# Two-batch macaron block on one core: later max and exponential units, and VectorE adding probability tiles ahead of the softmax sums

## The chip, the cores and the metric

The kernel runs on one core of a Trainium2 chip. The metric is the device time of one execution in microseconds (us); the kernel before is given as the median of three runs. TensorE does the matrix products, VectorE, ScalarE and GpSimd the work between them, and SyncE's queue issues the DMAs.

## The reference

Input x is (2, 1024, 512) in float32. Three residual steps follow each other: half a feed-forward step, attention, and another half feed-forward step, each on a layer-normalised x.

```python
x = x + 0.5 * ffn(layernorm(x), weight, bias, gamma, beta)   # inner layernorm, ternary weight
x = x + attn(layernorm(x), w_q, w_k, w_v, w_o)
x = x + 0.5 * ffn(layernorm(x), weight, bias, gamma, beta)

def attn(x, ...):                       # 16 heads of 32, rotary q and k
    scores = einsum('bhqd,bhkd->bhqk', q, k) / sqrt(32)
    scores = where(tok_mask, scores, -inf)     # causal in blocks of 64 tokens
    ctx = einsum('bhqk,bhkd->bhqd', softmax(scores), v)
    return ctx @ w_o.T
```

## The kernel before, in words

**Groups and runs.** The 16 heads of a batch form 4 groups of 4 heads, 8 groups in all. Every engine walks through one written-out loop over steps `k`; 48 steps make a run, and one run holds, side by side, one stage of three different groups:

- the q and k projections of group g (four parts of 12 steps, the products at their first ten steps, `L956`); ScalarE copies each result to `t1` one step after the last product (`L602`), GpSimd rotates it with four operations (`L502` twice, `L505`, `L507`), ScalarE and GpSimd split it into a high and a low half (`L623` at lag 8, `L511` at lag 9), and SyncE writes it to DRAM and reads it back into `qst` or `kst` (lags 11 and 14);
- the max pass of group g-1, "A units" from step `A_START` of the run on: 48 score products (`L939`), one a step, 12 for each head, each reduced over keys by VectorE (`L815`). They rotate through three PSUM banks (`a_bank`), so that a product waits until the unit three before it is reduced. After the twelfth unit of a head VectorE makes the max row with three small operations, each waiting for the one before: `L825` (min of two slices of `rmax`), `L827` (scaled high half) and `L828` (low half). I call these three **the max chain**. `MAX_PLACE` steps later TensorE transposes the result into one of the same three banks (`L1063`), ScalarE copies it one step later (`L617`), and a DMA puts it into `qst`. Around that place two A units have only two banks between them.
- the exponential pass of group g-2, "B units" from `B_START` on: 48 score products in transposed order (`L920`) over two banks, each turned into probabilities by ScalarE (`L609`). They form 12 steps of keys `st` with four heads each; `st` 0 to 3 belong to the first half of the queries and have 512, 384, 256 and 128 columns, `st` 4 to 7 to the second half with 512 columns each (the full tiles), `st` 8 to 11 again 512, 384, 256 and 128. `probs` has four places, so a tile lives for four values of `st`.

**Sums and contexts.** Five steps after its first unit (`SUM_LAG`), TensorE adds each `st` into the softmax sum with a ones matrix (`L1045`), for four heads in f32; nine steps after it (`PV_LAG`) it multiplies the same probabilities with v (`L1055`). So every fourth step has an f32 **block**: sums of one `st` and contexts of the one before. When the last `st` of a half is through, ScalarE takes the reciprocal by a logarithm and an exponential (`L629`, `L633`), VectorE multiplies (`L834`), and ScalarE and GpSimd split the result (`L641`, `L521`).

**Order.** Inside step k TensorE issues: B unit, A unit, projection, (other products), f32 block, transpose of the max row. VectorE issues: A reduction, then, where it is due, the max chain, then `L834`. Waits are on semaphores that count these operations. The third stage ends after 8 groups; the output products of batch 0 and its last feed-forward step are set between the last units, and those of batch 1 follow.

Of the kernel before, what the change touches and what calls it, by code (L numbers as in the profile page):

```python
# [17 lines left out]
F32 = mybir.dt.float32  # L18
# [29 lines left out]

STEPS = 48
ALL = BATCH * GROUPS  # L50
A_START, B_START = 10, 18
SUM_LAG, PV_LAG = 5, 9
P_PLACES = 4

SLOTS = [(0,), (1,), (2,), (3,), (4, 5), (6,), (7,), (8,), (9,), (10, 11)]
MAX_PLACE = 2
A_ORDER = [(i, half) for i in range(TILES) for half in range(i // 4 + 1)]
A_UNITS = len(A_ORDER)
B_ORDER = [(half, j) for half in range(BLOCKS) for j in range(4 * half + 4)]
# [7 lines left out]
def macaron(nc, x, w_q, w_k, w_v, w_o, w_f, bias, gamma, beta, cos_t, sin_t, ident_in, ident16_in,  # L67
            q_rows, k_rows, spread, out):
    ctx = ExitStack()
    with ctx:  # L70
# [69 lines left out]
        wf_s = flat(cl, None)  # L140
        wtg = xl[:, 0:2, :].rearrange("p a t -> p (a t)").rearrange("p (a b) -> p a b", a=4)

        x1_dram = [dram(f"x1_{b}", (P, TILES, C), F32) for b in range(BATCH)]
        xh_dram, xl_dram = dram("xh_1", (P, CC, T), F16), dram("xl_1", (P, CC, T), F16)
        ch_dram, cl_dram = dram("ch_0", (P, GROUPS, T), F16), dram("cl_0", (P, GROUPS, T), F16)
# [69 lines left out]
        s_qb = sem("s_qb")  # L215
        s_eb = sem("s_eb")
        s_sum = sem("s_sum")
        s_pv = sem("s_pv")
        s_ln = sem("s_ln")
        s_rec = sem("s_rec")  # L220
# [72 lines left out]
        def pv_step(k, lag):  # L293

            t = b_unit(k - lag)
            return (t[0], t[1], *t[3:]) if t and t[2] == 0 else None

        def ctx_half(k, lag=1):

# [23 lines left out]
        def _(sp):  # L323
# [64 lines left out]
            for k in range(LAST_STEP):  # L388
# [12 lines left out]
                if u := proj_after(k, 14):  # L401
# [4 lines left out]
                    if g >= SETS:  # L406
                        sp.wait_ge(s_qb, STEPS * (g - SETS + 1))
                    sp.dma_start(dst[0:MASK_ROW, g % SETS, :, cols],
                                 spread[n % 2].rearrange("a (d h) t -> (a d) h t", h=GH)).then_inc(s_stack[m], 16)
                if e := max_head(k, 4):  # L410
                    g, h = e
                    n = GH * g + h
                    sp.wait_ge(s_mrows, n + 1)
                    sp.dma_start(qst[MAX_ROW:ROWS_B, g % SETS, h, :], mrows[:, n % 2, :]).then_inc(s_mdma[h], 16)
# [113 lines left out]
        def _(act):  # L528
# [52 lines left out]
            for k in range(LAST_STEP):  # L581
# [21 lines left out]
                if t := b_unit(k):  # L603
                    g, st, h, half, j, q0, n = t
                    u = STEPS * g + GH * st + h
                    act.wait_ge(s_qb, u + 1)
                    if 12 * g + st >= P_PLACES:
                        act.wait_ge(s_pv, 12 * g + st + 1 - P_PLACES)
                    nc.scalar.activation(probs[:, st % P_PLACES, h, 0:n], pb[u % 2][:, 0:n], ACT.Exp,  # L609
                                         scale=EXP_SCALE).then_inc(s_eb, 1)  # L610
                if e := max_head(k, 3):
                    n = GH * e[0] + e[1]
                    act.wait_ge(s_mtr, n + 1)
                    if n >= 2:
                        g2, h2 = divmod(n - 2, GH)
                        act.wait_ge(s_mdma[h2], (g2 + 1) * 16)
                    nc.scalar.activation(mrows[:, n % 2, :], max_bank(n)[0:2 * TILES, 0:P // 2].bitcast(F16), ACT.Copy).then_inc(s_mrows, 1)  # L617
# [5 lines left out]
                    nc.scalar.activation(rhl[:, n % 2, 0, :], t1[:, n % 2, :], ACT.Copy).then_inc(s_rh, 1)  # L623
                if c := ctx_half(k, -4):
                    n = 2 * c[0] + c[1]
                    act.wait_ge(s_sum, 12 * c[0] + 4 + 8 * c[1])
                    if n:
                        act.wait_ge(s_cl, n)
                    nc.scalar.activation(cf[:, :], psum[:, :], ACT.Ln).then_inc(s_ln, 1)  # L629
# [16 lines left out]
        def _(dve):  # L646
# [126 lines left out]
            for k in range(LAST_STEP):  # L773
# [45 lines left out]
                if e := max_head(k, 0):  # L819
# [3 lines left out]
                    if n >= 2:  # L823
# [3 lines left out]
                    link(nc.vector.tensor_scalar(mparts[:, s, 0, :], rmax[:, at:at + 8], 1.0 / MAX_SCALE, None, ALU.mult))  # L827
                    nc.vector.scalar_tensor_tensor(mparts[:, s, 1, :], rmax[:, at:at + 8], 1.0 / MAX_SCALE,  # L828
                                                   mparts[:, s, 0, :], ALU.mult, ALU.subtract).then_inc(s_mp, 1)
                if c := ctx_half(k, 1):  # L830
                    n = 2 * c[0] + c[1]
                    dve.wait_ge(s_rec, n + 1)
                    dve.wait_ge(s_pv, 12 * c[0] + 4 + 8 * c[1])
                    nc.vector.scalar_tensor_tensor(cf[:, :], acc[:, :], CTX_SCALE, cf[:, :], ALU.mult, ALU.mult).then_inc(s_cf, 1)  # L834
# [20 lines left out]
        def _(pe):  # L855
# [52 lines left out]
            for k in range(LAST_STEP):  # L908
# [126 lines left out]
                if t := pv_step(k, SUM_LAG):  # L1035
                    g, st, half, j, q0, n = t
                    pe.wait_ge(s_eb, STEPS * g + GH * (st + 1))
                    if st == 0 and g % GROUPS == 0:
                        pe.wait_ge(s_vs[g // GROUPS], TILES)
                    if j == 0 and (g or half):  # L1040
                        pe.wait_ge(s_ln, 2 * g + half)
                    if g == 0 and st == 0:
                        pe.wait_ge(s_vs[1], TILES)
                    for h in range(GH):
                        last = nc.tensor.matmul(psum[h * D:(h + 1) * D, q0 - half * HALF:HALF], ones[:, 0:D],  # L1045
                                                probs[:, st % P_PLACES, h, 0:n], start=(j == 0), stop=(j == 4 * half + 3),
                                                skip_group_check=True)
                    last.then_inc(s_sum, 1)
                if t := pv_step(k, PV_LAG):
                    g, st, half, j, q0, n = t  # L1050
                    if j == 0 and (g or half):
# [8 lines left out]
                if e := max_head(k, MAX_PLACE):  # L1060
                    n = GH * e[0] + e[1]
                    pe.wait_ge(s_mp, n + 1)
                    nc.tensor.transpose(max_bank(n)[0:2 * TILES, 0:P // 2].bitcast(F16),  # L1063
                                        mparts[:, n % 2, :, :].rearrange("p a t -> p (a t)"),
                                        ident16[:, :]).then_inc(s_mtr, 1)
# [87 lines left out]
```

## Time and profile before

| what | value |
|---|---|
| median of 3 runs | 634.64 us (634.29 to 636.09) |
| the profiled execution | 634.23 us, its span 632.4 us |
| mean granted TensorE clock | 0.962 |
| TensorE busy | 554.8 us (88%) |
| VectorE busy | 396.8 us (63%) |
| ScalarE busy | 310.2 us (49%) |
| GpSimd busy | 238.5 us (38%) |

Busy is the time in which an engine had an instruction under way. Products are pipelined on TensorE, and the profile models their ends, so that the distance from one product's start to the next one's tells more of its cost than its own length. About 1.8 us of the execution lie around the span.

### The profile page before, as it was taken

To read this page: it belongs to the slowest core of one execution; us is meant where nothing else is said; L and a number is where in the kernel's file an instruction comes from. 1 tells how busy PE (TensorE), PEld (TensorE's weight loads), DVE (VectorE), ACT (ScalarE), POOL (GpSimd) and SP (SyncE) were. 2 spreads that over 40 slices of the span, in tenths; PEclk is the share of its full clock that TensorE was granted. 3 is DMA by queue.
4 is the path that set the end of the run, shared out by engine and by line. 5 is a ranking of instruction groups with operands and counts; after the bars stand their busy time and mean duration, and the time that the engine had idled before them with its cause. 6 is when DMAs were issued, how large, how long until landed. Compare 5 with 4: busy or idle time off the path is not lost.

```text
span 632.4 us, 10042 instructions
## 1 busy us (share of the span) xinstructions
PE 554.8 (88%) x3586; PEld 235.9 (37%) x3586; DVE 396.8 (63%) x782; ACT 310.2 (49%) x629; POOL 238.5 (38%) x200
## 2 busy tenths in 40 slices
PE   0695799679969999999999999999999898999876
PEld 0442445334423333333333333333333334344432
DVE  5899656626767757757757657657657843431672
ACT  0931632121215746746746746746736548572320
POOL 4001363443474646646646646646600100000100
PEclk9796899888989999999999999999999999999997
DMA  8921023354221215423213214514410003100011
GB/s 322 348 76 68 2 70 97 117 119 133 93 83 51 77 52 175 127 67 110 76 51 109 77 52 150 169 51 143 138 57 2 1 2 134 51 18 34 33 68 66
DMA packets 43601, 57.95 MB, mean 92 GB/s; under 512 B 3526, under 2 KB 34374, under 8 KB 42528
## 3 DMA queue, kind: packets, MB, share of 16 engines
q1 hardware_dynamic: 42972, 57.21, 27.6%
q8 instruction: 29, 0.48, 0.3%
q10 hardware_dynamic: 580, 0.11, 0.1%
q14 instruction: 20, 0.16, 0.1%
HBM read 32.01 MB, written 25.17 MB: 90 GB/s over the span
## 4 chain that ended last, share of the span: by engine, by line
PE 56%; DVE 19%; issue 8%; POOL 7%; DMA 7%; ACT 3%; SPq 1%; ACTq 0%; POOLq 0%; DVEq 0%
PE bank L956 9%; PE bank L874 7%; PE bank L939 7%; PE bank L920 7%; PE bank L1045 6%; PE bank L1055 5%; PE bank L884 5%; PE bank L993 5%; DMA kst<-spread 4%; DVE rmax L815 4%; DVE mparts L828 3%; DVE stats L661 3%; POOL rot L502 2%; DMA spread<-rhl 2%; PE bank L864 2%
## 5 line engine op out<-in xcount | busy, mean ns | idle before, releaser
L815 DVE TENSOR_REDUCE rmax<-bank 128x1 f32<-128x512 f32 (+3 forms) x384 | 200.9, 553 | 124.5 <-PE bank L939 121.5
L609 ACT ACTIVATE big<-bank 128x512 f32<-128x512 f32 (+3 forms) x384 | 182.0, 490 | 150.6 <-PE bank L920 145.7
L939 PE MATMUL bank<-kst,qst 104*128 104x512 f16 (+3 forms) x384 | 126.3, 330 | 15.3 <-issue 8.5
L920 PE MATMUL bank<-qst,kst 106*128 106x512 f16 (+3 forms) x384 | 123.9, 330 | 2.5 <-ACT big L609 2.2
L502 POOL TENSOR_TENSOR rot<-t,sin_s 64x512 f32<-64x512 f32 x64 | 81.8, 1277 | 96.3 <-ACT t L602 93.5
L1045 PE MATMUL bank<-big,ones 128*32 128x512 f32 (+3 forms) x768 | 81.8, 498 | 0.0
L1055 PE MATMUL bank<-big,rows 128*32 128x512 f32 (+3 forms) x768 | 79.5, 486 | 0.0
L920 PEld LDWEIGHTS bank<-qst,kst 106*128 106x128 f16 x384 | 37.1, 97 | 84.4 <-issue 41.4
L511 POOL TENSOR_TENSOR rhl<-t,rhl 128x512 f16<-128x512 f32 x32 | 37.5, 1171 | 70.9 <-ACT rhl L623 70.9
L521 POOL TENSOR_TENSOR cl<-cf,ch 128x512 f16<-128x512 f32 x16 | 18.6, 1160 | 112.3 <-ACT ch L641 112.3
L939 PEld LDWEIGHTS bank<-kst,qst 104*128 104x128 f16 x384 | 37.8, 98 | 51.2 <-issue 18.9
L956 PE MATMUL bank<-xh,wh 128*128 128x512 f16 x128 | 50.9, 401 | 6.4 <-DVE xl L697 5.9
L956 PE MATMUL bank<-xl,wh 128*128 128x512 f16 x128 | 44.9, 392 | 0.0
L461 POOL TENSOR_TENSOR rstd<-var_e,half_neg 128x4 f32<-128x4 f32 x12 | 13.0, 1084 | 83.5 <-DVE var_e L670 83.5
L956 PE MATMUL bank<-xh,wl 128*128 128x512 f16 x128 | 43.6, 381 | 0.0
L507 POOL TENSOR_TENSOR t<-t,rot 128x512 f32<-128x512 f32 x32 | 41.2, 1286 | 2.5
L505 POOL TENSOR_TENSOR t<-t,cos_s 128x512 f32<-128x512 f32 x32 | 40.9, 1280 | 2.5
L1055 PEld LDWEIGHTS bank<-big,rows 128*32 128x32 f32 x768 | 24.5, 110 | 37.5 <-issue 34.7
L690 DVE SCALAR_TENSOR_TENSOR rows<-bank,rows 128x512 f32<-128x512 f32 x24 | 16.3, 689 | 35.0 <-PE bank L874 34.8
L543 ACT ACTIVATE xh<-bank,bet,gam 128x512 f16<-128x512 f32 x24 | 18.9, 787 | 35.9 <-PE bank L864 35.9
L828 DVE SCALAR_TENSOR_TENSOR mparts<-rmax,mparts 128x8 f16<-128x8 f32 x32 | 34.6, 1081 | 1.1
L623 ACT ACTIVATE rhl<-t 128x512 f16<-128x512 f32 x32 | 20.0, 626 | 20.5 <-POOL t L507 20.5
(106 smaller groups left out, 667.9 us busy)
## 6 DMA issues: line engine op xcount, KB each, us to landing
spread<-rhl SPq DMA_DIRECT2D x32, 256.0 KB, 2.2
qst<-spread SPq DMA_DIRECT2D x16, 384.0 KB, 3.8
kst<-spread SPq DMA_DIRECT2D x16, 384.0 KB, 3.8
x<-rows SPq DMA_DIRECT2D x4, 1024.0 KB, 4.6
spread<-rhl SPq DMA_DIRECT2D x32, 128.0 KB, 2.1
rows<-in_L_attn_x_dram SPq DMA_DIRECT2D x3, 1024.0 KB, 15.5
xh<-ch SPq DMA_DIRECT2D x4, 512.0 KB, 4.6
xl<-cl SPq DMA_DIRECT2D x4, 512.0 KB, 6.2
```

The lines of the kernel that those rows point to most:

```text
L502: pool.tensor_tensor(rot[first:first + P // 2, n % 2, :], t1[other:other + P // 2, n % 2, :], sin_s[other:other + P // 2, cols], ALU.mult) ...
L505: pool.tensor_tensor(t1[:, n % 2, :], t1[:, n % 2, :], cos_s[:, cols], ALU.mult).then_inc(s_rot, 1)
L507: pool.tensor_tensor(t1[:, n % 2, :], t1[:, n % 2, :], rot[:, n % 2, :], ALU.add).then_inc(s_rope, 1)
L609: nc.scalar.activation(probs[:, st % P_PLACES, h, 0:n], pb[u % 2][:, 0:n], ACT.Exp, scale=EXP_SCALE).then_inc(s_eb, 1)
L815: nc.vector.tensor_reduce(rmax[:, at:at + 1], a_bank(u)[:, 0:n], AX.X, ALU.max, negate=True).then_inc(s_max, 1)
L828: nc.vector.scalar_tensor_tensor(mparts[:, s, 1, :], rmax[:, at:at + 8], 1.0 / MAX_SCALE, mparts[:, s, 0, :], ALU.mult, ALU.subtract).then ...
L874: last = nc.tensor.matmul(dst[:, :], (high, low)[a][:, cc, r * P:(r + 1) * P], wt[:, cc, :], start=False, stop=(n == 2 * CC))
L920: nc.tensor.matmul(pb[u % 2][:, 0:n], kst[0:ROWS_B, g % SETS, h, j * P:(j + 1) * P], qst[0:ROWS_B, g % SETS, h, q0:q0 + n], start=True, st ...
L939: nc.tensor.matmul(a_bank(u)[:, 0:n], qst[0:ROWS_A, g % SETS, h, i * P:(i + 1) * P], kst[0:ROWS_A, g % SETS, h, half * HALF:half * HALF + ...
L956: last = nc.tensor.matmul(pp[:, :], wp[ww][:, m % 2, cc, og * P:(og + 1) * P], xp[xw][:, cc, m // 2 * HALF:(m // 2 + 1) * HALF], start=(n ...
L1045: last = nc.tensor.matmul(psum[h * D:(h + 1) * D, q0 - half * HALF:HALF], ones[:, 0:D], probs[:, st % P_PLACES, h, 0:n], start=(j == 0), s ...
L1055: last = nc.tensor.matmul(acc[h * D:(h + 1) * D, q0 - half * HALF:HALF], rows[g // GROUPS][:, j, (GH * og + h) * D:(GH * og + h + 1) * D], ...
```

## The change

`A_START` goes from 10 to 11, `B_START` from 18 to 22, `MAX_PLACE` from 2 to 5. Of the full key tiles, `st` 4 and 5, and `st` 6 and 7, are added in pairs: VectorE writes probs[st] + probs[st+1] for each of the four heads (f32, 128 x 512) into `added`, which lies over the value weights that are no longer needed; the four additions of a pair come at lags 7, 8, 9 and 10 after the first unit of `st` 4 or 6. TensorE sums the totals instead of the four single tiles, at the lag of `st` 6 and of `st` 8. ScalarE waits for the additions before it overwrites their tiles.

```diff
-A_START, B_START = 10, 18
+A_START, B_START = 11, 22
+PAIRED = (4, 6)
+ADD_LAGS = (7, 8, 9, 10)
+SUMS = 10
-MAX_PLACE = 2
+MAX_PLACE = 5
+        added = [part[:, 2, :, :].rearrange("p c o -> p (c o)").bitcast(F32).rearrange("p (h n) -> p h n", h=2) for part in (wh, wl)]
+        def add_unit(k):
+            for h, lag in enumerate(ADD_LAGS):
+                s = pv_step(k, lag)
+                if s and s[1] in PAIRED:
+                    return s[0], PAIRED.index(s[1]), s[1], h
 # sync: max row out
-                if e := max_head(k, 4):
+                if e := max_head(k, MAX_PLACE + 2):
 # scalar
+                    if 4 <= st - P_PLACES < 8:
+                        act.wait_ge(s_add, 8 * g + 4 * ((st - P_PLACES - 4) // 2) + 4)
-                if e := max_head(k, 3):
+                if e := max_head(k, MAX_PLACE + 1):
-                    act.wait_ge(s_sum, 12 * c[0] + 4 + 8 * c[1])
+                    act.wait_ge(s_sum, SUMS * c[0] + 4 + (SUMS - 4) * c[1])
 # vector, behind the max chain of the step
+                if t := add_unit(k):
+                    g, p, st, h = t
+                    dve.wait_ge(s_eb, STEPS * g + GH * (st + 1) + h + 1)
+                    if g == 0 and p == 0:
+                        dve.wait_ge(s_vs[1], TILES)
+                    elif p == 0:
+                        dve.wait_ge(s_sum, SUMS * (g - 1) + 6)
+                    else:
+                        dve.wait_ge(s_sum, SUMS * g + 5)
+                    nc.vector.tensor_tensor(added[h // 2][:, h % 2, :], probs[:, st % P_PLACES, h, :],
+                                            probs[:, (st + 1) % P_PLACES, h, :], ALU.add).then_inc(s_add, 1)
 # tensor
-                    if j == 0 and (g or half):
-                        pe.wait_ge(s_ln, 2 * g + half)
-                    for h in range(GH):
-                        last = nc.tensor.matmul(psum[...], ones[:, 0:D], probs[:, st % P_PLACES, h, 0:n], start=(j == 0), ...)
-                    last.then_inc(s_sum, 1)
+                    if st - 2 in PAIRED:
+                        p = PAIRED.index(st - 2)
+                        pe.wait_ge(s_add, 8 * g + 4 * p + 4)
+                        if p == 0:
+                            pe.wait_ge(s_ln, 2 * g + 1)
+                        for h in range(GH):
+                            last = nc.tensor.matmul(psum[h * D:(h + 1) * D, :], ones[:, 0:D], added[h // 2][:, h % 2, :],
+                                                    start=(p == 0), stop=False, skip_group_check=True)
+                        last.then_inc(s_sum, 1)
+                    if st == 0 and g:
+                        pe.wait_ge(s_ln, 2 * g)
+                    if st < 4 or st >= 8:
+                        for h in range(GH):
+                            last = nc.tensor.matmul(psum[...], ones[:, 0:D], probs[:, st % P_PLACES, h, 0:n], start=(st == 0), ...)
+                        last.then_inc(s_sum, 1)
 # tensor, at the transpose of the max row
+                    if n + 1 < GH * ALL:
+                        pe.wait_ge(s_max, A_UNITS * (n + 1) + MAX_PLACE - 2)
```

## Rows read from the trace of the kernel before

**Rows 1.** Page, part 1: busy time, share, instructions.

```profile
PE 554.8 (88%) x3586; PEld 235.9 (37%) x3586; DVE 396.8 (63%) x782; ACT 310.2 (49%) x629; POOL 238.5 (38%) x200
```

**Rows 2.** Windows: PE, PEld, DVE, ACT, POOL busy; clock; DMA share; GB/s.

```profile
286.70:334.00 47.30, 45.55 (x342) 17.90 (x341) 32.03 (x63) 29.57 (x67) 27.19 (x22) 1.00 0.25 79
476.00:523.40 47.40, 45.28 (x339) 16.68 (x331) 31.12 (x72) 26.19 (x60) 3.34 (x3) 1.00 0.02 4
523.40:570.80 47.40, 45.24 (x307) 19.24 (x307) 17.02 (x32) 33.12 (x63) 3.34 (x3) 1.00 0.16 65
```

**Rows 3.** TensorE timeline, run 286.7 to 334: start us, length us, instruction, idle before.

```profile
286.92 0.38 PE L939 MATMUL bank<-kst,qst 104*128 104x512 f16 x1
287.14 0.59 PE L956 MATMUL bank<-xh,wl 128*128 128x512 f16 x2
287.57 0.33 PE L920 MATMUL bank<-qst,kst 106*128 106x384 f16 x1
287.74 0.22 PE L939 MATMUL bank<-kst,qst 104*128 104x128 f16 x1
...
289.05 0.40 PE L1055 MATMUL bank<-big,rows 128*32 128x128 f32 x8
289.80 0.22 PE L1063 MATMUL bank<-ident,mparts 128*16 128x128 f16 x1 [0.35 <-DVE mparts L828]
...
299.40 0.61 PE L1055 MATMUL bank<-big,rows 128*32 128x256 f32 x8
300.69 0.22 PE L1063 MATMUL bank<-ident,mparts 128*16 128x128 f16 x1 [0.67 <-DVE mparts L828]
...
307.34 1.07 PE L1045 MATMUL bank<-big,ones 128*32 128x512 f32 x8
308.22 1.04 PE L1055 MATMUL bank<-big,rows 128*32 128x512 f32 x8
309.20 0.39 PE L920 MATMUL bank<-qst,kst 106*128 106x512 f16 x1
...
328.01 0.38 PE L939 MATMUL bank<-kst,qst 104*128 104x512 f16 x1 [0.69 <-DMA kst<-spread]
```

**Rows 4.** VectorE timeline, same run.

```profile
286.68 1.35 DVE L815 TENSOR_REDUCE rmax<-bank 128x1 f32<-128x512 f32 x2 [0.99 <-PE bank L939]
288.06 0.16 DVE L825 TENSOR_TENSOR rmax<-rmax 128x4 f32<-128x4 f32 x1
288.26 0.17 DVE L827 TENSOR_SCALAR mparts<-rmax 128x8 f16<-128x8 f32 x1
288.46 1.28 DVE L828 SCALAR_TENSOR_TENSOR mparts<-rmax,mparts 128x8 f16<-128x8 f32 x1
...
290.97 0.68 DVE L834 SCALAR_TENSOR_TENSOR cf<-bank,cf 128x512 f32<-128x512 f32 x1
291.57 1.48 DVE L815 TENSOR_REDUCE rmax<-bank 128x1 f32<-128x512 f32 x3
...
333.97 0.69 DVE L815 TENSOR_REDUCE rmax<-bank 128x1 f32<-128x512 f32 x1 [0.99 <-PE bank L939]
```

**Rows 5.** ScalarE timeline, same run.

```profile
287.77 0.60 ACT L602 ACTIVATE t<-bank 128x512 f32<-128x512 f32 x1
```

**Rows 6.** GpSimd timeline, same run.

```profile
288.44 2.61 POOL L502 TENSOR_TENSOR rot<-t,sin_s 64x512 f32<-64x512 f32 x2 [2.65 <-ACT t L602]
```

**Rows 7.** Line L828 over the whole span: ns min/median/max, first and last start.

```profile
L828 DVE SCALAR_TENSOR_TENSOR mparts<-rmax,mparts x32: 168/1278/1290, 151.2 to 516.7; 128x8 f16<-128x8 f32 x32
```

**Rows 8.** VectorE timeline, 70 to 100 us.

```profile
77.12 1.03 DVE L684 TENSOR_TENSOR cl<-big,ch 128x512 f16<-128x512 f32 x1 [0.65 <-ACT big L544]
```

**Rows 9.** GpSimd timeline, 70 to 100 us.

```profile
74.49 3.11 POOL L502 TENSOR_TENSOR rot<-t,sin_s 64x512 f32<-64x512 f32 x2 [7.93 <-ACT t L602]
77.68 1.59 POOL L505 TENSOR_TENSOR t<-t,cos_s 128x512 f32<-128x512 f32 x1
```

**Rows 10.** VectorE timeline, 108 to 125 us.

```profile
117.37 5.81 DVE L676 TENSOR_SCALAR kst<-rows,mv,rstd 128x512 f32<-128x512 f32 x4 [1.21 <-POOL rstd L461]
```

More of the change, by code:

```diff
@@ L217, in macaron @@
         s_sum = sem("s_sum")
+        s_add = sem("s_add")
         s_pv = sem("s_pv")
@@ L1039, in _ @@
                         pe.wait_ge(s_vs[g // GROUPS], TILES)
-                    if j == 0 and (g or half):
-                        pe.wait_ge(s_ln, 2 * g + half)
                     if g == 0 and st == 0:
                         pe.wait_ge(s_vs[1], TILES)
-                    for h in range(GH):
-                        last = nc.tensor.matmul(psum[h * D:(h + 1) * D, q0 - half * HALF:HALF], ones[:, 0:D],
-                                                probs[:, st % P_PLACES, h, 0:n], start=(j == 0), stop=(j == 4 * half + 3),
-                                                skip_group_check=True)
-                    last.then_inc(s_sum, 1)
+                    if st - 2 in PAIRED:
[11 more added lines that the diff above has]
+                        for h in range(GH):
+                            last = nc.tensor.matmul(psum[h * D:(h + 1) * D, q0 - half * HALF:HALF], ones[:, 0:D],
+                                                    probs[:, st % P_PLACES, h, 0:n], start=(st == 0), stop=(j == 4 * half + 3),
+                                                    skip_group_check=True)
+                        last.then_inc(s_sum, 1)
                 if t := pv_step(k, PV_LAG):
```

## The prediction

> **What bounds the kernel now.** I read the page's totals first: TensorE is busy 88% of the span, VectorE 63%, GpSimd 38% [rows 1]. Then windows of one run each: from 192 us to 429 us the runs repeat, TensorE at 45.5 of 47.3 us and full clock, VectorE at 32, GpSimd at 27 [rows 2]. The same reduction comes back 47.29 us later (286.68, 333.97) [rows 4]. Six such runs hold B units of groups 0 to 5 beside projections; the last two B groups have no projection beside them, and GpSimd is idle there (3.3 us of 47.4) [rows 2].
>
> In the TensorE timeline nearly all starts follow each other without a hole: 0.22 us for 512 f16 columns (286.92 to 287.14), so 0.17, 0.11 and 0.06 for 384, 256 and 128, and 0.88 us for four f32 sums of 512 columns (307.34 to 308.22) [rows 3], 0.22 for each 128. I see two sorts of holes. The transpose of the max row waits for the max chain: the block part at 289.05 takes 0.22, the transpose starts at 289.80, a hole of 0.5; the one at 299.40 takes 0.44, the transpose is at 300.69, a hole of 0.85; the other two heads of the run have next to none. And one A unit waits 0.7 us for `kst` [rows 3]. A run has 2.1 us of holes, and else is TensorE work: 45.2 us.
>
> **Removed sums.** Four sums of 0.88 become two: -1.76 us a run of TensorE's own work, on the path.
>
> **Removed waits.** The transpose moves from two steps behind the last A unit to five, and over a further block: its 1.4 us go. `A_START` gives the `kst` DMA one more step of about 0.9 us: its 0.7 us go (the fixed chain from projection to landing isn't shortened; were it late again, up to 0.7 comes back). Together with the sums: -3.85 us a run, if nothing new is late.
>
> **The additions by themselves.** 128x512 f32 from two SBUF operands isn't in the trace; the nearest are the same operation with an f16 operand (L684) and L834, 0.68 us, the next instruction 0.60 after its start [rows 4]. I take 0.60; 8 a run are 4.8 us on an engine with 15 us free a run. As a sum this costs nothing. It is covered only where VectorE keeps within three A units of TensorE, so I look at the place.
>
> **What holds VectorE.** L828 handles 8 elements and takes 168 ns at the least, but 1278 in the median [rows 7]. At 288.46 it starts 20 ns after a GpSimd operation of 1.27 us (half of the 2.61 from 288.44 [rows 6]) and ends with it, at 289.74 [rows 4]. L684, a 512-column operation on two SBUF tensors, starts at 77.12 under a GpSimd operation that ends at 77.60, and ends 0.55 us behind that, at 78.15 [rows 8, 9]; the GpSimd operation that starts at 77.68 then takes 1.59 instead of 1.27 [rows 9]. Four L676 under the same GpSimd sequence take 5.81 us, one GpSimd operation each [rows 10]. L834 and L815, which read PSUM, aren't held (0.68 at 290.97, under GpSimd) [rows 4, 6]. So: a VectorE operation with two SBUF operands that starts under a GpSimd operation waits for its end, then streams.
>
> GpSimd's four rotations start with ScalarE's copy, one step behind the last projection product (287.77 + 0.60 + 0.07 = 288.44) [rows 5, 6], and last 5.3 us (four of 1.27, gaps of 0.08 [rows 9]). In the kernel before the first two operations of the max chain are through by then (288.06, 288.26) and only L828 is held [rows 4]. Afterwards the last A unit comes one step later against the projection, about 0.8 us (0.65 for the products of the step from 286.92, 0.17 for the next B unit) [rows 3]. L825 then starts 0.4 us inside the first rotation. It waits for its end (289.7), L827 slips in ahead of the second rotation (which comes after a gap of 0.08, while L827 is ready after 0.06: 0.02 as L828 ended behind the rotation, 0.04 as between L825's end and L827's start [rows 4, 6]), and L828 is held to the second one's end, about 291.1 instead of 289.74.
>
> L825 handles 4 elements, and in this trace it never meets a running rotation. The Trainium skill ("GPSIMD Engine Reference", section Key points) says that GpSimd shares its SBUF interfaces with VectorE and contends with instructions that have two SBUF inputs. By that L825 is held too; the trace bears the rule out for L684 and L828, and shows nothing for L825. By the rule the sum is the one below, without it that of the second rival.
>
> **The four head boundaries of a run.** I lay them out from step 12h+9's start, with the widths above, 0.1 us on either side of a block, ScalarE's copy and the rotations as read. The fourth A unit of the new head needs its first one reduced, and that stands behind the chain.
> - Head 0 to 1: TensorE could issue the fourth unit at 3.7 (block 0.7); last unit reduced 2.0, L825 held to 2.9, L828 to 4.2, first unit reduced 4.45: a hole of 0.75.
> - Head 1 to 2: the same with 3.55 against 4.4: 0.85.
> - Head 2 to 3, where the first pair's additions lie at the steps of the last two A units and of the first two new ones. From step 44's start: `L834` ends 1.67, unit 10 reduced 2.27, addition 0 at once (the rotation of 2.4 now waits for it and ends 4.1), unit 11 reduced 3.55, L825 held to 4.1, L828 to 5.45, addition 1 streams to 6.05, unit 0 reduced 6.3 (TensorE wanted it at 4.7: 1.6). Addition 2 is held by the third rotation to 7.7, unit 1 reduced 8.05 (TensorE at 7.0: 1.0), addition 3 held by the fourth to 9.3, and the pair's sums, ready at 8.5, wait 0.8 for it. Holes of 3.4.
> - Head 3 to 4: the second pair's additions meet only one GpSimd operation (L511), and the block there has two sums and a context, 2.6 us, which cover the chain but for 0.5.
>
> Together 5.5 us. From below: 2.5, if L825 isn't held and only the additions are; 0.8, if neither is (VectorE's own work at boundary 2). From above: L827 held as well adds one rotation, 1.35, at each of four boundaries: 10.9. I take 5.5, since L684 is the closest row to both operations.
>
> **Sum.** A run: -3.85 + 5.5 = +1.65, times six = +10. The two last B groups have no rotations: -1.76 each in windows where TensorE is busy 45.3 of 47.4 us [rows 2]: -3. At the start four more steps have A units without B units, where a step goes by the reduction's 0.69 instead of TensorE's 0.44 (1.0), and the chain is a little longer in the heads before: +1 in all; the four more steps at the end hold no new work. All other edits (SyncE's lag of the max row, ScalarE's waits for additions some ten steps old) have slack: cost 0; with the slack gone a late max row would hold the first B unit. Sum +8 on the profiled execution of 634.23: 642, where the median is 634.64.
>
> **Rivals.**
> 1. *The chain runs into the rotations and additions wait* (above): 642. Slower from holes of 4.2 us a run on (3.85 plus the ends' share). Its own range is 637 to 651.
> 2. *L825 isn't held, the additions are.* The chain ends as before, 0 at boundaries 0, 1 and 3, 2.2 at boundary 2 (0.2, 1.1 and 0.9 by the same list), 0.3 for the second pair: -3.85 + 2.5 = -1.35, times six -8, -3, +1: 624. For it: 4 elements. Against: L828's 8 are held.
> 3. *Nothing is held long* (TensorE's steps let VectorE meet gaps): -3.85 + 0.8 times six, -18, -3, +1: 614. Against it the order of L828 and the rotation, alike in most of its 32 places.
> 4. *It evens out*: holes of about 4.1 us a run, as with one addition less held: 634.
> 5. *L827 is held too*: +5.4 a run, 32 us more: 674. Against: it is ready 20 ns ahead of the rotation.
>
> **Numbers.** Chances: 0.47 for the first, 0.24 for the second, 0.12 for the third, 0.11 for the fourth, 0.06 for the fifth (slower). A part of the first's low end falls within 0.3%. A measurement of this kernel tells about 0.3% from no change: faster 0.37, within 0.12, slower 0.51. The range 615 to 651 leaves out the fifth and most of the third.
>
> **What the profile would show.** Of the six sums of 512 columns (L1045, times four heads) in a run, four are left; there are 64 additions. L825's mean well over 0.16 us, up to 1; L828's still over 1 in runs with GpSimd, and its end some 2.6 us behind the rotations' start. Additions of the first pair at 0.7 to 1.5 us, of the last two groups at 0.69. TensorE's waits: none for L828 at the transpose, none for `kst`; new ones for L815 at L939 and for the addition at L1045. Runs of about 49 us. I am wrong if L825 keeps 0.16 us under a running rotation, if `kst` is late again, or if runs come down to 44 us.

## The result and the profile after

664.46 us (median of 4, 664.25 to 668.63) against 634.46 us: 1.0492 times the time of the kernel before, 95% interval 1.0469 to 1.0516. Slower, as forecast, but by 30 us and not by 8, and above the range's upper end of 651. The rows below are from one profiled execution of each kernel (664.37 and 634.23 us).

The page of the changed kernel: totals, the clock's line of tenths by slice, the chain by engine, and the group of A units. (Lines have moved: `L967` is the A unit, `L948` the B unit, `L842`, `L844` and `L845` the max chain, `L856` the additions, `L1076` the sums of totals, `L1083` the other sums, `L1093` the contexts, `L517`, `L520`, `L522` the rotations, `L526` the split of the rotated tile, `L536` the context's low half.)

```profile
PE 556.7 (84%) x3458; PEld 233.9 (35%) x3458; DVE 457.9 (69%) x846; ACT 308.5 (47%) x629; POOL 251.5 (38%) x200
...
PEclk9897999789979899899899899899999899999798
...
PE 59%; DVE 29%; issue 6%; ACT 3%; DMA 1%; POOL 1%; SPq 0%; ACTq 0%; DVEq 0%; POOLq 0%
...
L967 PE MATMUL bank<-kst,qst 104*128 104x512 f16 (+3 forms) x384 | 126.5, 332 | 39.3 <-DVE rmax L832 32.3
```

Against [rows 1], VectorE's busy time went up by 61 us, though 64 additions at 0.69 are 44. TensorE's went up by 2 us though 128 of its instructions are gone, and in the steady part the clock's line has an 8 every third slice or so. A units wait 32 us for reductions.

One steady run, from a view of windows (PE, PEld, DVE, ACT, POOL busy, clock, DMA share, GB/s), and the two us at a time around its head boundary 2 to 3:

```profile
253.50:304.70 51.20, 45.87 (x328) 17.44 (x324) 40.67 (x70) 29.33 (x66) 29.31 (x23) 0.97 0.30 93
266.00:268.00 2.00, 0.61 (x3) 0.21 (x3) 2.00 (x4) 0.53 (x1) 1.92 (x2) 1.00 1.04 299
268.00:270.00 2.00, 0.83 (x4) 0.11 (x2) 2.00 (x3) 0.60 (x1) 1.92 (x3) 1.00 0.93 315
270.00:272.00 2.00, 1.42 (x9) 0.50 (x13) 2.00 (x4) 0.00 (x0) 1.49 (x1) 0.73 0.22 75
272.00:274.00 2.00, 2.00 (x14) 0.46 (x7) 0.14 (x1) 0.00 (x0) 0.00 (x0) 0.50 0.00 0
274.00:276.00 2.00, 2.00 (x10) 0.88 (x11) 0.85 (x2) 1.48 (x4) 0.00 (x0) 0.92 0.00 0
```

A run takes 51.2 us, not 47.3 [rows 2]. For four us VectorE and GpSimd are busy all the time and TensorE 1.44 us; then TensorE's clock goes down to half (1.2 GHz of 2.4) for 3.4 us. That happens once in each of the five runs that hold B groups 0 to 4. The DMA share near 1 in these rows isn't part of it: at the same boundary of the first of these runs (215 to 219 us) the share is 0.18, and TensorE is busy 1.43 us of the 4, with the clock at half behind it.

VectorE's and GpSimd's timelines there (start, length, instruction):

```profile
263.34 0.68 DVE L856 TENSOR_TENSOR wh<-big 128x512 f32<-128x512 f32 x1
263.94 0.68 DVE L832 TENSOR_REDUCE rmax<-bank 128x1 f32<-128x512 f32 x1
264.65 0.53 DVE L842 TENSOR_TENSOR rmax<-rmax 128x4 f32<-128x4 f32 x1
265.22 0.17 DVE L844 TENSOR_SCALAR mparts<-rmax 128x8 f16<-128x8 f32 x1
265.42 1.11 DVE L845 SCALAR_TENSOR_TENSOR mparts<-rmax,mparts 128x8 f16<-128x8 f32 x1
266.46 0.68 DVE L856 TENSOR_TENSOR wh<-big 128x512 f32<-128x512 f32 x1
267.06 0.28 DVE L832 TENSOR_REDUCE rmax<-bank 128x1 f32<-128x128 f32 x1
267.26 1.55 DVE L856 TENSOR_TENSOR wl<-big 128x512 f32<-128x512 f32 x1
268.73 0.41 DVE L832 TENSOR_REDUCE rmax<-bank 128x1 f32<-128x256 f32 x1
269.06 1.41 DVE L856 TENSOR_TENSOR wl<-big 128x512 f32<-128x512 f32 x1
```

```profile
263.43 3.08 POOL L517 TENSOR_TENSOR rot<-t,sin_s 64x512 f32<-64x512 f32 x2 [1.90 <-ACT t L617]
266.59 1.67 POOL L520 TENSOR_TENSOR t<-t,cos_s 128x512 f32<-128x512 f32 x1
268.34 1.59 POOL L522 TENSOR_TENSOR t<-t,rot 128x512 f32<-128x512 f32 x1
269.89 1.60 POOL L536 TENSOR_TENSOR cl<-cf,ch 128x512 f16<-128x512 f32 x1
```

`L842` has 4 elements and takes 0.53 us, until the first rotation ends; `L844` slips in; `L845` waits for the second; the third addition for the third, the fourth for the last one. GpSimd loses time in turn: the operations beside additions last about 1.6 us, where rotations take 1.27 and `L536` takes 1.16 elsewhere. And TensorE, from which one reads the bill:

```profile
265.52 0.38 PE L948 MATMUL bank<-qst,kst 106*128 106x512 f16 x1
267.39 0.39 PE L967 MATMUL bank<-kst,qst 104*128 104x512 f16 x1 [1.50 <-DVE rmax L832]
...
269.20 0.39 PE L967 MATMUL bank<-kst,qst 104*128 104x512 f16 x1 [0.98 <-DVE rmax L832]
...
270.58 0.79 PE L1076 MATMUL bank<-wh,ones 128*32 128x512 f32 x2 [0.78 <-issue]
...
271.95 2.01 PE L1093 MATMUL bank<-big,rows 128*32 128x512 f32 x8
273.66 0.31 PE L1103 MATMUL bank<-ident,mparts 128*16 128x128 f16 x1
```

Measured from start to start, less each product's own length at full clock, the holes are 1.66, 1.14 and 0.94 us. The contexts from 271.95 take 1.71 us where they take 0.88 elsewhere, the sums before them 1.37 instead of 0.85. The three holes, the slow stretch behind them (1.75 us in all) and the holes of the other boundaries (1.0, 1.1 and 0.8) are 8.4 us; the kernel before had 2.5 by the same measure. 8.4 - 2.5 - 1.76 of sums = +4.1; the run is 3.9 longer.

**Where the 30 us are.** From the starts of the B groups in both timelines, each group up to the start of the next: group 0 starts as before (189.8 against 189.7), groups 0 to 4 longer by 19.8, group 5 by 0.8, group 6 by 2.5, group 7 by 5.3 (62.3 against 57.0), and behind the last B unit 1.7 (55.1 against 53.4).

Group 5 is worth a look. The first pair meets the rotations there as in groups 0 to 4: `L842` 0.53, `L845` 1.11, additions of 1.55 and 1.42 us at 472.18 and 473.98. But the output products of batch 0 have taken the place of the projections, TensorE is busy 1.86 us of 4 (471.3 to 475.3) and not 1.44, it waits 1.06, 0.77 and 0.56 us and not 1.50, 0.98 and 0.78, and the clock stays at full speed. The group is 0.8 us longer, groups 0 to 4 are 3.8 to 4.3 us longer.

### The profile page after: what moved, and what is told of

It is laid out like the page before. It is cut to its first block, busy times and chain, and to the rows that moved or that the text cites. A ratio compares the mean times of both kernels' runs of the same rounds, so it can differ in the third digit from the quotient of the medians.

```text
span 662.6 us, 9960 instructions
## 1 busy us (share of the span) xinstructions
PE 556.7 (84%) x3458; PEld 233.9 (35%) x3458; DVE 457.9 (69%) x846; ACT 308.5 (47%) x629; POOL 251.5 (38%) x200
## 4 chain that ended last, share of the span: by engine, by line
PE 59%; DVE 29%; issue 6%; ACT 3%; DMA 1%; POOL 1%; SPq 0%; ACTq 0%; DVEq 0%; POOLq 0%
PE bank L984 9%; PE bank L1093 8%; PE bank L967 7%; PE bank L948 7%; DVE rmax L832 7%; PE bank L902 6%; PE bank L912 6%; PE bank L1083 6%; PE bank L1021 5%; DVE stats L678 3%; PE bank L1076 3%; DVE mparts L845 3%; DVE wl L856 3%; DVE rmax L842 3%; PE bank L892 2%
## 5 line engine op out<-in xcount | busy, mean ns | idle before, releaser
L832 DVE TENSOR_REDUCE rmax<-bank 128x1 f32<-128x512 f32 (+3 forms) x384 | 199.5, 550 | 89.4 <-PE bank L967 88.2
L967 PE MATMUL bank<-kst,qst 104*128 104x512 f16 (+3 forms) x384 | 126.5, 332 | 39.3 <-DVE rmax L832 32.3
L948 PE MATMUL bank<-qst,kst 106*128 106x512 f16 (+3 forms) x384 | 127.5, 334 | 3.6 <-ACT big L626 3.3
L517 POOL TENSOR_TENSOR rot<-t,sin_s 64x512 f32<-64x512 f32 x64 | 86.3, 1348 | 82.2 <-ACT t L617 79.5
L1093 PE MATMUL bank<-big,rows 128*32 128x512 f32 (+3 forms) x768 | 85.7, 516 | 1.4 <-DVE cf L862 1.4
L526 POOL TENSOR_TENSOR rhl<-t,rhl 128x512 f16<-128x512 f32 x32 | 38.5, 1204 | 90.7 <-ACT rhl L640 90.7
L948 PEld LDWEIGHTS bank<-qst,kst 106*128 106x128 f16 x384 | 37.1, 97 | 94.7 <-ACT big L626 35.7
L967 PEld LDWEIGHTS bank<-kst,qst 104*128 104x128 f16 x384 | 38.0, 99 | 86.5 <-DVE rmax L832 43.4
L536 POOL TENSOR_TENSOR cl<-cf,ch 128x512 f16<-128x512 f32 x16 | 21.8, 1365 | 99.0 <-ACT ch L658 99.0
L1083 PE MATMUL bank<-big,ones 128*32 128x128 f32 (+3 forms) x512 | 47.7, 443 | 0.0
L520 POOL TENSOR_TENSOR t<-t,cos_s 128x512 f32<-128x512 f32 x32 | 43.3, 1354 | 2.5
L522 POOL TENSOR_TENSOR t<-t,rot 128x512 f32<-128x512 f32 x32 | 43.0, 1344 | 2.5
L1093 PEld LDWEIGHTS bank<-big,rows 128*32 128x32 f32 x768 | 24.0, 113 | 34.8 <-issue 31.6
L617 ACT ACTIVATE t<-bank 128x512 f32<-128x512 f32 x32 | 19.1, 598 | 26.9 <-PE bank L984 26.6
L845 DVE SCALAR_TENSOR_TENSOR mparts<-rmax,mparts 128x8 f16<-128x8 f32 x32 | 30.9, 965 | 1.1
```

The costliest lines, as they stand in the source:

```text
L517: pool.tensor_tensor(rot[first:first + P // 2, n % 2, :], t1[other:other + P // 2, n % 2, :], sin_s[other:other + P // 2, cols], ALU.mult) ...
L520: pool.tensor_tensor(t1[:, n % 2, :], t1[:, n % 2, :], cos_s[:, cols], ALU.mult).then_inc(s_rot, 1)
L522: pool.tensor_tensor(t1[:, n % 2, :], t1[:, n % 2, :], rot[:, n % 2, :], ALU.add).then_inc(s_rope, 1)
L832: nc.vector.tensor_reduce(rmax[:, at:at + 1], a_bank(u)[:, 0:n], AX.X, ALU.max, negate=True).then_inc(s_max, 1)
L948: nc.tensor.matmul(pb[u % 2][:, 0:n], kst[0:ROWS_B, g % SETS, h, j * P:(j + 1) * P], qst[0:ROWS_B, g % SETS, h, q0:q0 + n], start=True, st ...
L967: nc.tensor.matmul(a_bank(u)[:, 0:n], qst[0:ROWS_A, g % SETS, h, i * P:(i + 1) * P], kst[0:ROWS_A, g % SETS, h, half * HALF:half * HALF + ...
```

## The experiments

The diffs show the lines that carry each edit; counters and waits that follow from them are left out. A ratio is to the kernel before, with its 95% interval.

The held theory says: VectorE operations on two SBUF tensors wait for GpSimd's operations; that, above all where the first pair's additions stand beside the rotations, opens TensorE's holes, and the clock goes down behind them. Its rivals: the additions cost by their own length (work); the three new places cost by themselves (place).

### One part of the change alone

`e1_shift_only`: the kernel before with the three places.

```diff
-A_START, B_START = 10, 18
+A_START, B_START = 11, 22
-MAX_PLACE = 2
+MAX_PLACE = 5
```

> The kernel before with the three new places (A units at 11, B units at 22, the max row's transpose five steps behind) and no additions. Held theory (VectorE operations with two SBUF operands wait for GpSimd's rotations; most of the loss is in the additions beside them, and in TensorE's clock after the holes): L825 is held as in the changed kernel (0.7 us in the mean), holes of about 1.8 us a run instead of 2.5, no step down of the clock in the steady runs, a run of 46.6 us, about 630 us in all. Place theory (the new places alone cost the time): 650 us or more, runs near 51 us.

637.6 us, 1.0048 (1.0031 to 1.0065). Its runs are as expected, 46.9 us, with holes of 0.81 and 1.02 us and the clock up; `L825` is held 0.8 us in the median:

```profile
L825 DVE TENSOR_TENSOR rmax<-rmax x32: 161/802/969, 150.5 to 511.4; 128x4 f32<-128x4 f32 x32
```

The place theory falls, but the total missed: what the runs gain is lost ahead of the first B group (1.2 us), in the last group and behind it (2.9 and 1.9), the latter two for the reason that `e8_late_tail` tests.

`e2_adds_only`: the changed kernel with the old places.

```diff
-A_START, B_START = 11, 22
+A_START, B_START = 10, 18
-MAX_PLACE = 5
+MAX_PLACE = 2
```

> The changed kernel with the old places (10, 18 and 2): additions and the sums of totals alone. The first pair's additions then lie between two rotations, the second pair's first two lie under the rotations' end. Held theory: L825 is back at 0.16 us, additions of the first pair at 0.69 but for one, two of the second pair at 1.0 to 1.5; holes of 3 to 4 us a run, a run of 46 to 47 us, 625 to 636 us in all. Work theory (VectorE's 64 additions cost by their own length, wherever they stand): as the changed kernel, 660 us or more.

637.75 us, 1.0053 (1.0032 to 1.0073), just above the expected 625 to 636 and far from 660: the same additions cost 27 us less at these steps, so the work theory falls. They aren't free there either: two waits of 0.69 and 1.15 us a run stand behind the first pair, for the reason that `e7_clear` shows. This kernel also prices the clock. Most of its steady runs keep it up, two don't. The same boundary in two runs (windows: PE, PEld, DVE, ACT, POOL busy, clock), and the contexts in it:

```profile
310.00:320.00 10.00, 7.62 (x48) 2.65 (x46) 9.53 (x16) 4.80 (x10) 5.88 (x5) 1.00 0.23 74
...
358.00:368.00 10.00, 8.15 (x44) 2.44 (x43) 8.62 (x15) 4.04 (x9) 5.46 (x5) 0.83 0.19 61
```

```profile
313.97 1.07 PE L1093 MATMUL bank<-big,rows 128*32 128x512 f32 x8
315.57 0.22 PE L1103 MATMUL bank<-ident,mparts 128*16 128x128 f16 x1 [0.54 <-DVE mparts L845]
...
362.37 1.87 PE L1093 MATMUL bank<-big,rows 128*32 128x512 f32 x8
364.06 0.22 PE L1103 MATMUL bank<-ident,mparts 128*16 128x128 f16 x1
```

With the clock at half the contexts need 1.7 us; at full clock a wait for the max chain lay behind them and hides part of it, so the run is 0.8 us longer (48.4 against 47.6). The waits are the same in both (0.69 and 1.15 us; 0.70 and 1.15). `e7_clear` has such a case too: of its runs with B groups 0 to 4 only the one of group 4 has the clock at half, for 3.4 us, behind the same waits, and it takes 48.8 us where groups 1 to 3 take 47.2 to 47.9.

`e12_after_second_pair`: the changed kernel without the first pair.

```diff
-PAIRED = (4, 6)
+PAIRED = (6,)
-                    if st < 4 or st >= 8:
+                    if st < 6 or st >= 8:
```

> The changed kernel, places and all, with the first pair left out: st 4 and 5 are summed one by one, only st 6 and 7 are added, at the lags of the changed kernel. If the first pair's additions beside the rotations (3.7 us of holes) and the clock's step behind them (1.75) carry the loss, a run has 0.9 of sums more and 5 us of stalls less: 46.5 to 47.5 us, clock up, 636 to 642 us in all. If the loss lies in both pairs alike, a run stays near 49 us.

637.58 us, 1.0045 (1.0030 to 1.0061), runs of 46.8 us at full clock, as expected: leaving out four additions a group, and doing one more tile's sum on TensorE for it, gives back 27 us. The loss is the first pair's, at these steps.

### Taking the conflict away

`e3_short_rot`: the changed kernel with short rotations; the rotary embedding is left out for 448 of 512 columns of each part. `e6_before_short_rot` is the same edit in the kernel before.

```diff
-pool.tensor_tensor(t1[:, n % 2, :], t1[:, n % 2, :], cos_s[:, cols], ALU.mult)
+pool.tensor_tensor(t1[:, n % 2, 0:64], t1[:, n % 2, 0:64], cos_s[:, cols.start:cols.start + 64], ALU.mult)
```

> The changed kernel with GpSimd's four rotation operations on 64 of 512 columns each; this leaves out the rotary embedding of the other columns. VectorE's work is untouched. Held theory: L825 at 0.16, additions near 0.7, next to no holes at the head boundaries, no step down of the clock in steady runs, a run of 43.5 to 44.5 us and 620 to 630 us in all. Work theory: 655 us or more, since no VectorE operation is removed.

> The kernel before with GpSimd's four rotation operations on 64 of 512 columns, which leaves out the rotary embedding of the other columns: the control for the same edit in the changed kernel. Held theory: L828 is at 0.17, the transposes' waits and the kst wait go (2.5 us of holes a run), a run of 45 us and about 618 us; so the changed kernel with the same edit (623 us) is still no faster than the kernel before with it. If the rotations cost the kernel before nothing, it stays at 634.

623.3 us and 615.69 us. The shorter rotations are worth 41 us to the changed kernel and 19 to the one before. Not all of that is in the runs: the first B group starts 7.8 us earlier in `e3_short_rot` and 9.9 in `e6_before_short_rot`. A steady run gets 5.7 us shorter in the changed kernel (51.2 to 45.5) and 1.5 in the one before (47.3 to 45.8). VectorE's max chain and additions in `e3_short_rot`:

```profile
L842 DVE TENSOR_TENSOR rmax<-rmax x32: 161/163/399, 145.2 to 496.0; 128x4 f32<-128x4 f32 x32
...
L856 DVE TENSOR_TENSOR wl<-big x32: 674/675/1440, 205.0 to 547.7; 128x512 f32<-128x512 f32 x32
```

`L842` is no longer held; some additions still are, mostly by `L526`'s and `L536`'s operations, which I left long. The clock stays up in the steady runs. They take 45.5 us, not the 43.5 to 44.5 expected: 2.9 us of holes stay, behind those additions. With short rotations in both kernels, the change's runs are hardly shorter (45.5 against 45.8), and its end is longer. The control missed in part: `L828` is at 0.32 us in the median, not 0.17, still held to the end of the shortened operation, and the `kst` waits stay (3.4 us in four waits from 225 to 409 us); only the transposes' waits are gone.

`e4_no_adds`: the changed kernel with the totals set once to a constant; the full key tiles are missing in the softmax sums.

```diff
-                if t := add_unit(k):
+                if (t := add_unit(k)) and t[0] == 0 and t[1] == 0:
-                    nc.vector.tensor_tensor(added[h // 2][:, h % 2, :], probs[...], probs[...], ALU.add).then_inc(s_add, 1)
+                    nc.vector.memset(added[h // 2][:, h % 2, :], 1.0).then_inc(s_add, 1)
```

> The changed kernel without VectorE's additions: the totals are set once to a constant, so the softmax sums leave out the full key tiles. TensorE does all that it does in the changed kernel. Held theory: the max chain is still held by the rotations, so holes of 1.0 and 0.8 us at two boundaries stay and 0.5 at the third; no step down of the clock, a run of 45.3 us, about 620 us. Place theory: 650 us or more.

632.86 us, 0.9967 (0.9946 to 0.9988). Runs of 45.6 us at full clock, holes of 0.81, 1.02 and 0.61 us: as expected to 0.3 us. The total isn't (620 expected): the last B group takes 63 us and the part behind it 55, as in the changed kernel, so these losses aren't the additions'. They aren't the places' alone either, since `e1_shift_only` has 59.9 for the 63.

`e5_a10`: the changed kernel with the A units back at 10.

```diff
-A_START, B_START = 11, 22
+A_START, B_START = 10, 22
```

> The changed kernel with the A units at 10, as before; B units stay at 22 and the transpose at five steps. The max chain stands ahead of the rotations again, while the first pair's additions still stand beside them, at the boundary of heads 2 and 3. If holding L825 were most of the loss, holes would go down to about 3 us a run, the clock would stay up and runs come to 46 us, about 635 us. If the additions under the rotations are most of it, the holes at that one boundary stay near 3.5 us with the clock's step behind them, and only the 1.8 us of the other boundaries go, less a wait for the kst DMA that comes back (0.9): runs of 49 to 50 us, 648 to 656 us in all.

683.03 us, 1.0781 (1.0730 to 1.0831), worse than either branch of the expectation. The holes at the boundary of heads 2 and 3 are not 3.5 but 5.8 us, by the same measure, and the clock is at half for 6.8 or 10.2 us a run instead of 3.4, here from 324.6 to 334.8 (windows of a run, and within its boundary):

```profile
286.10:339.60 53.50, 48.56 (x327) 17.39 (x324) 39.63 (x71) 29.34 (x66) 28.52 (x22) 0.90 0.22 70
...
322.00:328.00 6.00, 2.50 (x8) 0.54 (x7) 6.00 (x8) 1.43 (x3) 5.79 (x4) 0.72 0.21 66
328.00:330.00 2.00, 1.20 (x7) 0.33 (x10) 1.89 (x4) 0.74 (x2) 0.00 (x0) 0.50 0.00 0
```

The premise failed at this boundary: `L842` starts 0.16 us behind the rotation and is held 1.14 us, in every steady run; only at two of the four boundaries is it back at 0.16. So the run doesn't price the holding of the chain by itself. The additions' steps follow the B units, the reductions' the A units. With A one step earlier all four additions come ahead of, or among, the reductions that TensorE needs next, and the transpose waits as well. What is held, and how long, turns on single steps.

This kernel also has `L844` held, which escapes in all 32 places of the changed kernel. At 193.72 a rotation started 10 ns ahead of `L844`, which reads one SBUF tensor of 8 elements:

```profile
193.52 0.16 DVE L842 TENSOR_TENSOR rmax<-rmax 128x4 f32<-128x4 f32 x1
193.72 1.29 DVE L844 TENSOR_SCALAR mparts<-rmax 128x8 f16<-128x8 f32 x1
...
193.71 2.63 POOL L517 TENSOR_TENSOR rot<-t,sin_s 64x512 f32<-64x512 f32 x2 [3.67 <-ACT t L617]
```

It is held like the others (1.29 us for 0.17), so the hold isn't confined to operations on two SBUF tensors; in the changed kernel `L844` escapes because it starts first.

### The end of the kernel

`e8_late_tail`: `e1_shift_only` with the output products and the last feed-forward step of batch 0 four steps later.

```diff
-O0_START = STEPS * ALL
+O0_START = STEPS * ALL + 4
```

> The kernel with the new places and no additions (637.6 us), with all work of the output products and the last feed-forward step of batch 0 set four steps later as well, so that it stands to the last B units as it did in the kernel before. If the loss of the last two groups and the end comes from that work standing four steps earlier against the B units, the last B group goes from 59.9 us to 57 and the end behind it from 55.3 to 53.4: 631 to 634 us. If the shift of the B units by itself costs the end, 637 us.

633.94 us, 0.9996 (0.9975 to 1.0016), as expected. The last B group and the part behind it, in `e1_shift_only` and then here:

```profile
520.10:580.00 59.90, 56.96 (x393) 23.77 (x394) 19.74 (x35) 36.01 (x70) 3.59 (x3) 1.00 0.17 63
580.00:635.30 55.30, 41.40 (x200) 18.55 (x198) 25.43 (x52) 13.06 (x20) 3.17 (x3) 0.91 0.13 48
```

```profile
521.80:578.80 57.00, 54.84 (x386) 23.10 (x385) 19.10 (x35) 35.73 (x70) 3.34 (x3) 1.00 0.17 61
578.80:632.20 53.40, 41.55 (x209) 18.79 (x207) 25.96 (x53) 13.04 (x20) 3.17 (x3) 0.94 0.15 54
```

Both are back at the 57.0 and 53.4 us of the kernel before. The same edit in the changed kernel is `e11_after_late_tail`.

> The changed kernel with the output products and the last feed-forward step of batch 0 set four steps later, so that they stand to the last B units as before. If the 5.3 us that the last B group loses and the 1.7 us behind it come from the distance between these and the B units (as 2.9 and 1.9 did without additions), it gains 5 to 7 us: 657 to 660 us, steady runs unchanged at 51.2 us. If additions in the last groups cost them, it stays at 662 to 665 us.

658.86 us, 1.0387 (1.0362 to 1.0413), 5.6 us less than the changed kernel. Its last B group takes 55.3 us instead of 62.3, the part behind it 53.0 instead of 55.1, steady runs still 51.2; that was expected. Group 5 loses 2.2 us more instead: with the output products four steps later the clock goes to half there too, from 473.0 us on, for 6.8 us. In the changed kernel one sees where the end was long: TensorE waits 3.5 us for the last context.

```profile
613.27 0.42 PE L1093 MATMUL bank<-big,rows 128*32 128x128 f32 x8
617.21 1.89 PE L912 MATMUL bank<-wh,ch 128*128 128x512 f16 x4 [3.52 <-POOL cl L536]
```

and in the middle of the last group the normalised rows came late (2.17 us at 578.43, for VectorE's `L693`), each time with the clock at half close behind. In `e11_after_late_tail` the first wait is 1.5 us, as in the kernel before, and the second is gone. That less of batch 0's work was left beside the last context fits this.

### Versions

`e7_clear`: the old places, transpose five steps behind, the second pair's additions at lags 11 to 14, so that both pairs stand at steps 5 to 8 of 12.

```diff
-ADD_LAGS = (7, 8, 9, 10)
+ADD_LAGS = ((7, 8, 9, 10), (11, 12, 13, 14))
-                    if st - 2 in PAIRED:
+                    if st in (6, 9):
```

> A version with the additions clear of the rotations: places 10 and 18 as before, transpose five steps behind, the first pair's additions at lags 7 to 10 and the second pair's at 11 to 14, so that both lie at steps 5 to 8 of 12, between two rotations; the second pair's sums go with st 9. Held theory: additions near 0.69 but for the one that meets L511, L825 at 0.16, holes of 1 to 2 us a run (the kst DMA among them), clock up, a run of 44.5 to 45.5 us, 616 to 624 us in all. Work theory: no gain over the kernel before, 634 us or more.

638.08 us, 1.0069 (1.0044 to 1.0094), where 616 to 624 were expected: a miss. GpSimd isn't idle between the rotations where the first pair stands: behind `L511`'s operation the context's low half runs, which I had left out of the count (`L527`, `L537`, then the next rotation, `L518`):

```profile
303.18 1.40 POOL L527 TENSOR_TENSOR rhl<-t,rhl 128x512 f16<-128x512 f32 x1 [1.02 <-ACT rhl L641]
304.54 1.60 POOL L537 TENSOR_TENSOR cl<-cf,ch 128x512 f16<-128x512 f32 x1
306.88 2.94 POOL L518 TENSOR_TENSOR rot<-t,sin_s 64x512 f32<-64x512 f32 x2 [0.73 <-ACT t L618]
```

Three additions of four are held there, and holes of 0.86 and 1.33 us follow; the second pair leaves one of 0.27.

`e9_one_pair`: `e7_clear` without its first pair.

```diff
-PAIRED = (4, 6)
-ADD_LAGS = ((7, 8, 9, 10), (11, 12, 13, 14))
+PAIRED = (6,)
+ADD_LAGS = ((11, 12, 13, 14),)
```

> Places 10 and 18 as before, transpose five steps behind, and only st 6 and 7 are added, at lags 11 to 14, where GpSimd has one operation (L511's) in their way; st 4 and 5 are summed one by one again, so no addition stands beside the low half of the context and the rotation behind it. Held theory: the holes in the two-pair version behind its first pair (0.9 and 1.3 us a run) go, the sum saves 0.88 us a run, the kst wait of 0.9 stays; a run of 45 to 45.8 us, 620 to 626 us in all. If additions cost by being there, it is no better than the kernel before (634).

625.35 us, 0.9861 (0.9834 to 0.9888), as expected (620 to 626): 1.4% less than the kernel before, clear of noise. Against `e10_place5` below, which has the same places, the second pair alone is worth 9.3 us. One run:

```profile
272.40:318.40 46.00, 45.52 (x335) 17.35 (x333) 34.80 (x67) 29.84 (x66) 27.26 (x22) 1.00 0.25 82
```

`e10_place5`: the kernel before with the later transpose alone.

```diff
-MAX_PLACE = 2
+MAX_PLACE = 5
```

> The kernel before with the transpose five steps behind the last A unit and nothing else. The max chain ends as before with the first rotation operation, so no A unit waits for it, and the transposes' holes (1.4 to 1.6 us a run) go: a run of 45.7 to 46.3 us, 624 to 628 us in all. If the holes only move (to the A unit that needs the first bank, or to the kst wait), a run stays at 47 us and the time at 632 to 636 us.

634.64 us, 1.0004 (0.9982 to 1.0025). The second branch: the transposes' holes go, and a run stays at 47.3 us or so. Around one of them:

```profile
338.35 0.38 PE L956 MATMUL bank<-xh,wh 128*128 128x512 f16 x1
338.66 0.22 PE L1065 MATMUL bank<-ident,mparts 128*16 128x128 f16 x1
338.81 0.28 PE L920 MATMUL bank<-qst,kst 106*128 106x256 f16 x1
339.48 0.23 PE L939 MATMUL bank<-kst,qst 104*128 104x128 f16 x1 [0.38 <-DVE rmax L815]
```

The transpose now stands one step away from the f32 block, and costs two gaps of 0.1 us of its own, four times a run, and one A unit waits 0.56 us behind it, where two banks serve. The `kst` wait is still there (0.83 us in this run, at 327.94).

## Why the prediction was wrong in size and right in kind

- **L825 is held, L827 slips in, L828 is held to the second rotation.** Right: 0.80, 0.17 and 1.11 us in the median. The rule of the Trainium skill on two SBUF inputs ("GPSIMD Engine Reference", section Key points), which decided between the first two rivals, holds in the trace for 4 elements too; `e3_short_rot` shows the hold going with the rotation's length. The working's own rule, "a VectorE operation with two SBUF operands", was too narrow for its rows: `L676` reads one SBUF tensor and two scalars a partition, and was held all the same, and `L844` was in `e5_a10`.
- **The boundary of heads 2 and 3.** Right nearly to a tenth: from step 44's start at 261.08, the two A units came at 6.3 and 8.1 us (6.3 and 8.05 forecast), the sums at 9.5 (9.3). Holes of 3.7 for 3.4.
- **The other boundaries.** 0.81 and 1.02 for 0.75 and 0.85, and 1.1 for 0.5 at the fourth, where the chain met the second rotation too. Holes were 6.7 for 5.5, against 2.5 instead of 2.1 before: 1.2 and -0.4 us a run against the forecast.
- **The step that failed first: the run's sum, "-3.85 + 5.5".** It priced TensorE's work at full clock and had no term for what the holes do to the clock: that term stood at nothing. Each steady run has 3.4 us at half clock behind its largest holes, 1.75 us a run. Five such runs are 8.75 of the 22 us missing. The steady runs before stood at full clock [rows 2], and nothing in the text asked whether it would stay. "Times six" was wrong too: five runs took 3.8 to 4.3 us more, and the sixth, at full clock, 0.8.
- **The step that failed second: "the four more steps at the end hold no new work", and the -3 for the last two groups.** They lost 7.8 us instead of gaining 3, and 1.7 behind them. The output and feed-forward work of batch 0 stands at fixed steps; moving the B units four steps against it changed which engine is late, with 4.8 us in `e1_shift_only` (2.9 and 1.9), all of which `e8_late_tail` gives back in these two stretches (and loses 1.4 of it in group 6). `e11_after_late_tail` gives back 9.1 there in the changed kernel (7.0 and 2.1), and 5.6 in all. The places alone explain 4.8 of the 7.0 us that the changed kernel loses in these two stretches (5.3 and 1.7); where the rest comes from is open.
- The parts: steady groups 20.6 for 10, last groups +7.8 for -3, end 1.7 for 0, start 0.1 for 1 (1.2 in `e1_shift_only`): 30.2 for 8.
- **Removed waits.** Right: no transposes wait for L828 and none for `kst` in the steady runs.
- The fifth rival (674) was nearer in time, and wrong in its mechanism: `L844` takes 0.17 us in all 32 places of the changed kernel. The nearness is luck.
- Why group 6 loses 2.5 us, where no rotation runs, I have not taken apart; a hole of 2.55 us before an A unit at 518.57, behind VectorE's output update and statistics (514.12 to 517.9), is the largest piece, with the clock at half for 3.4 us behind it. The longest such wait there was 1.3 us in the kernel before.

## What to carry to other kernels

Count an added operation with what the other engine runs at that very step: here the same eight additions made a run 0.3 us (`e2_adds_only`) or 3.9 us longer by the step at which they stood, and the price is read off the start times of both engines' timelines, not off busy shares. Look along that engine's whole queue there, not only at its largest sequence: `e7_clear` missed by two shorter operations. When a forecast has TensorE idle several us in a short stretch, add a term for the clock behind it. And a shift of one pipeline against work at fixed steps is a change of its own: list what stood beside its first and last steps.

## What the runs showed of the hardware

- A VectorE operation on two SBUF tensors that starts some 20 ns behind a GpSimd operation of 1.27 us ends with it: `L842`, 4 elements, takes 1.28 us instead of 0.16. One that starts ahead isn't held: the addition at 263.34 begins 0.09 us ahead of the rotation and takes its usual 0.68 us. GpSimd then runs about 1.6 us instead of 1.27 beside a 512-column addition.
- An operation on one SBUF tensor can be held as well: `L844`, 0.17 us in all 32 cases of the changed kernel, where it always starts first, takes 1.29 in `e5_a10` at 193.72, where the rotation starts 10 ns ahead of it. `L832`, which reads PSUM, isn't held (0.68 us at 263.94).
- TensorE's clock went to half for 3.4 us behind a stretch in which TensorE was busy 1.44 us of 4. It stayed up in group 5 of the same execution, with 1.86 us of 4, and in `e12_after_second_pair`, whose holes are 2.9 us but spread over a run. In `e2_adds_only` and `e7_clear` the same holes brought it down in some runs and not in others.
